# Rounding the feed-forward activations by counting thresholds, with narrower PSUM slots, in a fused attention and ternary feed-forward kernel on eight cores

## The reference

```
u  = LN(x) @ W_in.T + b_in
h_t = exp(lambda_log) * h_{t-1} + gamma * u_t          # scan over 2048 steps
x  = x + LN(h @ W_out.T + b_out + LN(x))
# feed-forward: 1024 -> 4096 -> 1024
q(a) = clip(round(a * 127/max|a|), -128, 127) / (127/max|a|)   # per row
w(W) = clip(round(W/s), -1, 1) * s,  s = mean|W|
x  = x + LN( q(gelu(q(LN(x)) @ w(W1).T)) @ w(W2).T )
```

## Time and profile before

| | us |
|---|---|
| median of 9 runs | 4545.7 |
| lowest and highest of the 9 | 4492.6 and 4669.98 |
| the profiled execution's own time | 4496.73 |
| its span, slowest core (core 5) | 4495.2 |
| spans of the eight cores | 4462.6 to 4495.2 |
| VectorE busy / TensorE busy in that span | 2940.8 / 2782.5 |

### The profile page before, as it was taken

How to read it: one execution, slowest core, us unless ns; L and a number is a source line. 1 busy time by engine, 2 the same in 40 slices (tenths; PEclk the granted TensorE clock), 3 DMA queues, 4 the chain that set the end, 5 groups by cost and what they waited for, 6 DMA issues and landing times. The chain is left out here.

```text
span 4495.2 us, 39784 instructions; the slowest of 8 cores (4462.6 to 4495.2 us)
## 1 busy us (share of the span) xinstructions
PE 2782.5 (62%) x12080; PEld 1550.0 (34%) x12080; DVE 2940.8 (65%) x2628; ACT 1584.5 (35%) x1797; POOL 201.5 (4%) x372
## 2 busy tenths in 40 slices
PE   5565554555566355454454454454554299999998
PEld 4444444444455222222222222221221144444444
DVE  4767777777777468888888888888887422223222
ACT  1333333333344344444444444444444211111111
POOL 0000000000000000000000000000000000000000
PEclk7776776777777677777777777777777699999999
DMA  4332346666411311211212212212212356666665
GB/s 132 113 113 89 119 128 155 150 166 160 119 56 56 113 44 57 65 56 60 63 55 63 63 52 66 63 52 66 63 52 66 125 139 150 152 153 153 152 155 127
DMA packets 537179, 447.28 MB, mean 100 GB/s; under 512 B 473206, under 2 KB 473208, under 8 KB 524424
## 3 DMA queue, kind: packets, MB, share of 16 engines
q1 hardware_dynamic: 479624, 184.58, 19.5%
q0 software_dynamic: 57344, 260.15, 16.7%
HBM read 193.02 MB, written 151.00 MB: 77 GB/s over the span
## 5 line engine op out<-in xcount | busy, mean ns | idle before, releaser
L914 PE MATMUL ps_h<-w1T,qdT 128*128 128x512 bf16 x4096 | 1005.7, 411 | 1003.1 <-DMA qdT<-qd 1003.1
L914 PEld LDWEIGHTS ps_h<-w1T,qdT 128*128 128x128 bf16 x4096 | 423.0, 104 | 1585.8 <-issue 1183.3
L1026 PE MATMUL ps_f<-w2T,qhT 128*128 128x512 bf16 x4096 | 887.0, 380 | 70.7 <-DMA qhT<-qhscr 70.7
L1026 PEld LDWEIGHTS ps_f<-w2T,qhT 128*128 128x128 bf16 x4096 | 401.4, 98 | 556.4 <-issue 75.0
L148 ACT ACTIVATE h_b<-ps_h,zerov,g3s 128x1024 f32<-128x1024 f32 x256 | 308.4, 1204 | 660.1 <-PE ps_h L914 660.1
L737 PE MATMUL ps_u<-lnT,winT 128*128 128x256 f32 x2048 | 394.8, 375 | 225.5 <-ACT gu L148 187.8
L148 DVE BATCH_NORM_STATS2 bn<-ffn 128x6 f32<-128x512 f32 x128 | 88.8, 694 | 577.6 <-ACT ffn L148 570.6
L737 PEld LDWEIGHTS ps_u<-lnT,winT 128*128 128x128 f32 x2048 | 381.6, 285 | 245.1 <-issue 242.8
L148 DVE TENSOR_TENSOR bh<-y0h,r16h 128x4096 bf16<-128x4096 f32 x64 | 283.2, 4425 | 208.9 <-ACT r16h L148 208.9
L148 ACT ACTIVATE y0h<-h_b,halfv,sch_all 128x4096 f32<-128x4096 f32 x64 | 243.2, 3801 | 359.2 <-DVE sch_all L148 359.2
L148 DVE TENSOR_REDUCE amh<-h_b 128x1 f32<-128x4096 f32 x64 | 282.9, 4420 | 124.8 <-ACT h_b L148 124.8
(11 more groups left out here) (99 smaller groups left out, 2333.4 us busy)
## 6 DMA issues: line engine op xcount, KB each, us to landing
qstg<-w SPq DMA_DIRECT2D x64, 1024.0 KB, 6.4
qhscr<-qh_b POOLq DMA_DIRECT2D x64, 1024.0 KB, 5.1
x_buf<-x POOLq DMA_DIRECT2D x32, 1024.0 KB, 6.3
r2scr<-r2b POOLq DMA_DIRECT2D x64, 512.0 KB, 3.0
r2B<-r2scr POOLq DMA_DIRECT2D x64, 512.0 KB, 5.8
r2C<-r2scr POOLq DMA_DIRECT2D x64, 512.0 KB, 5.7
y<-outb POOLq DMA_DIRECT2D x64, 512.0 KB, 3.4
w1tscr<-wtp SPq DMA_DIRECT2D x32, 256.0 KB, 3.1
```

Source lines behind the costliest of these rows:

```text
L914: last = t.matmul(pslot, qdTv[ta % 2][:, j, :], w1v[:, j, 512 * hs:512 * (hs + 1)], start=(j == 0), stop=(j == DT - 1))
L1026: last = t.matmul(pslice, qhTv[ta % 2][:, j, :], w2v[:, j, 512 * half:512 * (half + 1)], start=(j == 0), stop=(j == HT - 1))
```

## The change

The correction of the wide tile is written in another way, and the PSUM buffers of block B1 are cut differently. Before, VectorE compared `y0h` with `r16h` twice (is the value below the integer, is it at least one above), subtracted the two answers, and added that to the integer less 385. Now it takes the difference `y0h - r16h` (as bf16), counts how many of the ten thresholds -4 to 5 lie at or below it, one instruction for each threshold (the first writes the count `ch`, the other nine add to it), and adds the count to the integer less 390. `dcorr`, the narrow correction, stays as it was.

The four PSUM buffers of 1024 columns become six of 512; the gelu becomes eight instructions of 512 columns a tile in place of four of 1024, and the counts in the waits on `s_gel` follow (TensorE waits for the gelu six pieces back, the reduce for eight gelus a tile). On the host, the output array takes the type of the first core's result.

```diff
+    QK = 5
...
-            ps_h = [p1.enter_context(nc.psum_tensor(f"ps_h{i}", [128, 1024], F32))
-                    for i in range(4)]
+            ps_h = [p1.enter_context(nc.psum_tensor(f"ps_h{i}", [128, 512], F32))
+                    for i in range(6)]
...
-                    v.wait_ge(sem("s_gel"), (HS // 2) * (ta + 1))
+                    v.wait_ge(sem("s_gel"), HS * ta + HS)
...
                     v.wait_ge(sem("s_r16h"), ta + 1)
                     v.tensor_tensor(bh[:], y0h[ta % 2][:], r16h[ta % 2][:],
-                                    op=ALU.is_lt)
-                    v.scalar_tensor_tensor(ch[:], y0h[ta % 2][:], 1.0,
-                                           r16h[ta % 2][:],
-                                           op0=ALU.subtract, op1=ALU.is_ge)
-                    v.tensor_tensor(bh[:], ch[:], bh[:], op=ALU.subtract)
+                                    op=ALU.subtract)
+                    v.tensor_scalar(ch[:], bh[:], float(-QK + 1), None,
+                                    op0=ALU.is_ge)
+                    for tau in [float(k) for k in range(-QK + 2, QK + 1)]:
+                        v.scalar_tensor_tensor(ch[:], bh[:], tau, ch[:],
+                                               op0=ALU.is_ge, op1=ALU.add)
                     if ta >= 2:
                         v.wait_ge(sem(f"s_qhd{ta % 2}"), 16 * (ta // 2))
                     iqh = v.scalar_tensor_tensor(qh_b[ta % 2][:], r16h[ta % 2][:],
-                                                 385.0, bh[:],
+                                                 385.0 + QK, ch[:],
                                                  op0=ALU.subtract, op1=ALU.add)
...
-                        for hp in range(HS // 2):
-                            q = HS * tb + 2 * hp
-                            a.wait_ge(sem("s_h3"), q + 2)
-                            ig = a.activation(h_b[:, 1024 * hp:1024 * (hp + 1)],
-                                              ps_h[(q // 2) % 4][:], AF.Gelu,
+                        for hs in range(HS):
+                            q = HS * tb + hs
+                            a.wait_ge(sem("s_h3"), q + 1)
+                            ig = a.activation(h_b[:, 512 * hs:512 * (hs + 1)],
+                                              ps_h[q % 6][:], AF.Gelu,
...
-                        if q >= 8:
-                            t.wait_ge(sem("s_gel"), q // 2 - 3)
+                        if q >= 6:
+                            t.wait_ge(sem("s_gel"), q - 5)
                         last = None
-                        pslot = ps_h[(q // 2) % 4][:, 512 * (q % 2):512 * (q % 2 + 1)]
                         for j in range(DT):
-                            last = t.matmul(pslot,
+                            last = t.matmul(ps_h[q % 6][:],
...
-    out = np.empty((Bf, Lf, Df), dtype=np.float32)
+    r0 = np.asarray(res.results[0]["y"])
+    out = np.empty((Bf, Lf, Df), dtype=r0.dtype)
```

More of the change, by code:

```diff
@@ L1068 @@
     res = run_bass_kernel_spmd(nc, in_maps, core_ids=list(range(NCORES)))
-    out = np.empty((Bf, Lf, Df), dtype=np.float32)
+    r0 = np.asarray(res.results[0]["y"])
+    out = np.empty((Bf, Lf, Df), dtype=r0.dtype)
     for c in range(NCORES):
         out[c * nb:(c + 1) * nb] = np.asarray(
-            res.results[c]["y"], dtype=np.float32).reshape(nb, Lf, Df)
+            res.results[c]["y"]).reshape(nb, Lf, Df)
     return out
```

## The result

The changed kernel takes 6649.15 us (median of 12 executions, 6643.24 to 6837.07), the kernel before 4541.76 (median of 39). Some executions are a few per cent longer, at a lower granted clock on one die or both: medians hold them, ratios leave them out, and without them the kernel before is near its profiled execution's 4497. The ratio is 1.477, 95% interval 1.472 to 1.483: clearly slower. The forecast was 6675 us, with a range of 6600 to 6790. The profiled execution took 6647.16 us on its own time (span 6645.6, core 3); the sum for it had been 6652.

What follows compares the result with a forecast made beforehand. Block B1 was taken as bound by the chain through TensorE; the wide correction, 15.98 to 51.22 us, makes VectorE set 64.40 us a tile. Adding 2155.7 to 4496.7 gives 6652, with half of 49 more 6675 us; range 6600 to 6790.

Steps and rivals of the forecast that it cites:

- the sum for it: Whole kernel: 2155.7 us added in block B1 to the profiled execution's 4496.7, giving 6652 us.
- The difference: VectorE's wide correction: `y0h` less `r16h` costs as the comparison it replaces, a step of 4.53 us.
- the first threshold: VectorE's wide correction: one-input bf16 instruction, 4096 wide, taken at 1.29 us; rival cases 2.35 or 4.43, chance 0.05.
- the nine: VectorE's wide correction: nine scalar-tensor-tensor thresholds at 4.43 us each, steps of 4.53, together 40.77 us.
- The choice between 2.29 and 4.43: Nine thresholds on VectorE: forecast 4.43 us each; rival, bf16 rate of 2.29, whole kernel 5444 us, chance 0.08.
- The slack: VectorE in block B1: about 1.6 us a tile to spare; anything beyond lengthens the tile one for one.
- The edits at nothing: Block B1's PSUM buffers, gelu pieces and waits, and the host output type: no cost, under a cover of 34 us.
- the 27 us feared: TensorE's burst after long idle: 27 us in place of 15.6 if all 64 matmuls ran at the lower clock.
- carrying over half of the 49 us: Whole kernel: middle between 6652 and 6701 us, as the profiled execution lay 49 us under the median; gives 6675.
- other-side rival: Block B1: not slower, TensorE chain stays the bound, shorter last gelu saves 27 us, 4469 us; chance 0.01.
- this chain sets the tile, step for step: Block B1 before: reduce, narrow correction, transpose, matmuls, gelu, reduce set the tile, 30.74 us over the block.

Runs made afterwards that it cites:

- two-instruction run: Changed kernel, each of the nine further thresholds as a one-input comparison and a two-input add, not one scalar-tensor-tensor: 6194.06 us, ratio 1.381.
- third run: Kernel before with the PSUM change alone, narrow correction's two-input difference and second comparison left out: 4422.96 us for its profiled execution, ratio 0.987.
- first run: Kernel before with the PSUM change alone, clamp of the row maximum left out: 4505.64 us, ratio 1.000.
- a fifth: Kernel before with the PSUM change alone, narrow correction's two-input difference left out: 4477.84 us for its profiled execution, no ratio on record.

## Why the prediction was right

- *Which instruction costs what.* The difference was counted at 4.43 us and took 4.43; the first threshold at 1.29 (extrapolated from 32-bit rows and a factor of two) and took 1.227; the nine at 4.43 and took 4.425. The 1.29 was an estimate from two extrapolations, and its 0.06 us were 4 us of the sum. The tile was forecast at 64.40 us and is 64.39 on the mean: an ordinary one takes 64.34, and a few have a gap like the 0.46 us in the one shown. That the two errors nearly cancel is luck, of a size that matters little. The choice between 2.29 and 4.43 carried 1230 us, and the row that decided it was `qh_b`: all operands of 16 bits, no gain.
- *The Trainium skill's rule against it.* The sentence of Vector Engine (DVE) Microarchitecture Reference, section 7, Points that are easy to get wrong, by which two non-bf16 sources halve this form's rate, finds no support: with two bf16 sources it takes 4425 ns, with one 4425, with none 4425. Section 5.1 of that page of the Trainium skill, which does not list this form among those that pack, is what the runs show, and the two-instruction run shows that those which it does list do gain (1227 and 2292 ns).
- *The slack.* VectorE had 1.6 us a tile to spare and pays one for one after that: two thresholds cost nothing, four cost 37.21 - 30.74 = 6.47 us a tile (forecast 6.42), ten 33.65.
- *The edits at nothing.* The PSUM change in and out of the changed kernel makes no difference (6649.15 and 6648.89), and a doubled burst does not lengthen the tile. The 512-wide gelu takes 777 ns, forecast 778. TensorE's burst after 49 us of idle was 15.74 us, not the 27 feared.
- *What was off.* The step of carrying over half of the 49 us between the profiled execution and the median: the median after lies 2 us above its profiled execution. The sum itself, 6652, was 3 us from the median, and 5 from the profiled execution, whose first reduce started 7 us sooner than the sum had it.
- *A step that failed in the other-side rival.* It priced the shorter last gelu at 0.43 us a tile on the chain, 27 us. Alone it gives nothing, as the later rise of the clock within the burst takes it back. The rival was not the case, so the forecast didn't depend on it; but the reading "this chain sets the tile, step for step" was too simple in the downward direction, and in the kernel before small gains on that chain would have been predicted wrong.

## What to carry to other kernels

When a pass over a wide tile is added, first ask what slack the engine has in that stage, and then price the pass from the row with the same form and the same operand widths: scalar-tensor-tensor took 4.43 us for 4096 elements here with each of the three pairs of input types, and comparing and adding in two instructions took 3.52. Before making a correction cheaper, ask whether it is needed: leaving the rounding to the conversion and taking the transposed operand off the chain brought the block from 30.7 to 15.4 us a tile (whether the conversion's rounding will do is a question for the numbers, not for the profile). A chain with a burst of matmuls in it need not shorten by what is taken off it; look at idle and burst of TensorE together. And work taken off an engine that waits beside it for another comes back as wait: the third run took 2.13 us off the narrow correction, and VectorE waited 2.1 us more for `r16h`.

## What was not expected of the hardware

In kernels whose tile is set by the chain through TensorE, the rises of its clock stood 30.7 us apart on the mean in four kernels whose chains differ by up to 0.7 us (before, PSUM change, two thresholds, first run), and in most tiles of a fifth at 1.2. Three successive rises of the kernel before, for instance, 61.3 us from the first to the last:

```profile
2007.41 11.77 PEld L914 LDWEIGHTS ps_h<-w1T,qdT 128*128 128x128 bf16 x55 [0.28 <-issue]
2038.02 11.82 PEld L914 LDWEIGHTS ps_h<-w1T,qdT 128*128 128x128 bf16 x55 [0.28 <-issue]
2068.71 11.84 PEld L914 LDWEIGHTS ps_h<-w1T,qdT 128*128 128x128 bf16 x55 [0.28 <-issue]
```

The gain came back as a longer stretch at 1.2 GHz, 3.4 to 5.9 us of each burst. In the third run, whose tile of 29.2 us VectorE and ScalarE set, the rises don't follow that tile: the two shown stand 27.24 us apart (2087.07 - 2059.83), and the bursts are uneven. In the kernel with four thresholds, where VectorE sets 37.2 us, and in the changed kernel, such bursts lie under VectorE and cost nothing (15.74 us in the tile shown).
